# Attention of the chosen tokens: three rows of scores, six places for turned weights, and the products with V in every second head

## The chip, the cores and the metric

The kernel runs on one core of one Trainium2 chip. The metric is device time in microseconds (us) of one execution. Engines are TensorE (PE; PEld is its weight load), VectorE (DVE), ScalarE (ACT), GpSimd (POOL) and SyncE (SP).

## What is computed

One input `x` of 8192 rows by 512 goes through a layer norm; two branches work on the result and are added to `x`. The first is an attention over segments of 64 rows that carries a memory matrix from one segment to the next. The second picks the best eighth of the rows (1023 of 1024 are used) and runs a transformer block on these alone. What the change touches is the attention inside that block:

```python
q = rope(heads(hn @ wq), pos_sel)
kk = rope(heads(hn @ wk), pos_sel)
v = heads(hn @ wv)
sc = jnp.einsum('bhqd,bhkd->bhqk', q, kk) / np.sqrt(hd).astype(np.float32)
sc = sc + m_sel[:, None]
a = jax.nn.softmax(sc, axis=-1)
o = jnp.einsum('bhqk,bhkd->bhqd', a, v).transpose(0, 2, 1, 3).reshape(b, kc, d) @ wo
x1 = x_sel + o
```

There are 16 heads of 32 columns and 1023 chosen rows, padded to 1024. The multilayer perceptron of the block, with `w1` and `w2`, follows.

## The kernel before

The program has three parts one after the other: the segment attention, the chosen rows' attention with its preparation, and the perceptron. The part changed is the loop over chosen rows, from 1458.9 us to about 1808 us. Its buffers are declared from line 1743 on, its five engine programs follow until line 2127, and `mlp` comes after it.

The 1024 query rows are 8 tiles of 128 (`t` = 0 to 7), and each tile runs over 16 heads (`h`), 128 steps in all. All 1024 keys are handled at once for one head. One step is spread over three engines, each with its order written out by hand in its own `heads` function. Below, "head h" of an engine is what that engine does in iteration h of its own loop.

- TensorE, `heads` at line 2085, in this order: `score(t, h + 2)`, two products of 512 columns into the PSUM pair `Sp[h % 2]` (line 2011); then, in some heads, half of a product with V; then `turn_p(t, h - 1)`, eight transposes of the weights of head h-1 into two PSUM banks, four into `Tp[0]` (line 2019) and four into `Tp[1]` (line 2023); then, in some heads, one further piece.
- `values` is the product of four heads' turned weights with V, in two halves (`part` 0 and 1) of 32 small products each (line 2037). Group g of a tile is heads 4g to 4g+3. The halves come in heads 4g+5 and 4g+6, so two heads with products are followed by two without. Group 3 of a tile comes in heads 1 and 2 of the next one.
- The further pieces of TensorE are for the tile before: `back` in head 3, `again` in head 5 (four transposes each), `project` in head 7 (eight products of 512 columns with `wo`, line 2060), `norm_t` in head 15; and for the tile to come `stack` in heads 9, 10, 11 and 13 (four transposes each, line 2081), which makes the next tile's queries.
- VectorE, `heads` at line 1957: the reduce of head h (line 1965), which adds the mask columns to the scores, writes a row of `Sm` and takes its minimum into `least`, and then `take_t(t, h - 2)`, the copy of `Tp[1]` into a place of `PTs` (line 1916). In some heads one piece follows the copy: `weights` in head 1, `attention_rows` in head 4, `stack` in head 5 (line 1922), `second_norm` in five steps in heads 8 to 12. In the last tile `keep` comes in heads 0 to 5 and 13.
- ScalarE, `heads` at line 1861: the exponential of head h in place in `Sm` (line 1864), `take_o`, `take_t(t, h - 1)`, the copy of `Tp[0]` into `PTs` (line 1837), and in some heads a piece: `take_x1`, `take_on` in head 6, `stack` in head 3 (line 1845), `take_stack` in heads 9, 10, 11 and 13.

The waits that tie them: `score(t, h + 2)` waits until VectorE has reduced head h, since it writes over the same PSUM pair; the reduce waits for its scores and until the row of `Sm` is turned; the transposes wait for the exponential and until the copies before have emptied `Tp`; the copies wait for the transposes, and for `values` to have released their place in `PTs`:

```python
def read_before(eng, t, h):
    n = t * H + h - SLOTS
    if n >= 0:
        eng.wait_ge(s_pv, n // 4 + 1)
```

`Sm` has 4 rows of 4 KB in each partition, and `PTs` has 5 places of 4 KB. GpSimd gathers each tile's mask columns ahead by DMA, and SyncE loads the first perceptron weights during the last tile.

Of the kernel before, what the change touches and what calls it, by code (L numbers as in the profile page):

```python
# [12 lines left out]
ALU = mybir.AluOpType  # L13
ACT = mybir.ActivationFunctionType
# [10 lines left out]
P = 128  # L25
# [1227 lines left out]
def feed_forward(nc, x, maskT, positions, router_w, router_b, wq_d, wk_d, wv_d, wo_d, w1_d, w2_d, ln1, ln2,  # L1253
# [5 lines left out]
    H, DK = 16, 32  # L1259
    Q = idx.shape[1]  # L1260
    K = Q * P
    G = D // P
# [13 lines left out]
    with ExitStack() as ctx:  # L1276
        def sb(name, shape, dt=F32, c=ctx):
            return c.enter_context(nc.sbuf_tensor(name, shape, dt))
# [4 lines left out]
        ident = sb("ident2", [P, P])  # L1283
# [24 lines left out]
        mc = mcr[:, :, :].bitcast(F32)  # L1308
# [433 lines left out]
        up = Up(nc, ctx, KS, QS, xs2, x1T, Sp, w1_d, w2_d)  # L1742
        with ExitStack() as c2_:
            wo = sb("wo2", [P, G, D], c=c2_)
            Sm = sb("Sm", [P, 4, K], c=c2_)
            least = sb("least", [P, 4], c=c2_)
            rsum = sb("rsum", [P, 2, H], c=c2_)
            rinv = sb("rinv", [P, H], c=c2_)
            SLOTS = 5
            PTs = sb("PTs", [P, SLOTS, Q, P], c=c2_)  # L1750
            OTs = sb("OTs", [P, G, P], c=c2_)
            On = sb("On", [P, D], c=c2_)
# [36 lines left out]

            def slot(t, h):  # L1790
                return (t * H + h) % SLOTS

            def read_before(eng, t, h):

# [37 lines left out]
            @block.scalar  # L1832
            def _(act):
                def take_t(t, h):
                    act.wait_ge(s_t, t * (2 * H) + (2 * h + 1))
                    read_before(act, t, h)
                    act.activation(PTs[:, slot(t, h), 0:4, :], Tp[0][:, :].rearrange("p (k q) -> p k q", k=4),  # L1837
                                   ACT.Copy).then_inc(s_ta, 1)

                def take_o(t, g):  # L1840
                    act.wait_ge(s_pv, t * G + (g + 1))
                    act.activation(OTs[:, g, :], Op[:, 0:P], ACT.Copy).then_inc(s_oc, 1)

                def stack(t):
                    act.activation(qst[:, :, 0:2, :], q_rows(t), ACT.Copy).then_inc(s_qh, 1)

                def take_stack(t, g):
                    act.wait_ge(s_qp, t * G + (g + 1))
                    act.activation(QS[:, 4 * g:4 * g + 4, :], Wp[:, :].rearrange("p (h k) -> p h k", h=4),
                                   ACT.Copy).then_inc(s_qs, 1)  # L1850

                def take_on(t):
                    act.wait_ge(s_ot, t + 1)
                    act.activation(OnT[:, :, :], Wp[:, :].rearrange("p (g k) -> p g k", g=G), ACT.Copy).then_inc(s_otc, 1)

                def take_x1(t):
                    act.wait_ge(s_h2t, t + 1)
                    act.activation(x1T[:, :, cols(t)], Wp[:, :].rearrange("p (g k) -> p g k", g=G),
                                   ACT.Copy).then_inc(s_x1, 1)

                def heads(t, b, before=True, after=True):
                    for h in range(H):
                        act.wait_ge(s_sm, t * H + (h + 2))
                        act.activation(Sm[:, h % 4, 0:KC], Sm[:, h % 4, 0:KC], ACT.Exp, bias=least[:, h % 4:h % 4 + 1],  # L1864
                                       scale=-1.0, accum_out=rsum[:, b, h:h + 1]).then_inc(s_e, 1)
                        if h == 2 and before:
                            take_o(t - 1, G - 1)
                        if h in (6, 10, 14):
                            take_o(t, h // 4 - 1)
                        if h > 0:  # L1870
                            take_t(t, h - 1)
                        elif before:
                            take_t(t - 1, H - 1)
                        if h == 1 and before and t >= 2:
                            take_x1(t - 2)
                        if h == 6 and before:
                            take_on(t - 1)
                        if h == 3 and after:
                            stack(t + 1)
                        if h in (9, 10, 11, 13) and after:  # L1880
                            take_stack(t + 1, min(h - 9, 3))

                act.sem_inc(s_ta, 1)
                act.sem_inc(s_oc, 1)
                act.sem_inc(s_qh, 1)
                act.sem_inc(s_qs, G)
                heads(0, 0, before=False)
                for t in range(1, Q):
                    heads(t, t % 2, after=t < Q - 1)
                act.wait_ge(s_s, Q * H)  # L1890
                up.high(act, 0)
                take_t(Q - 1, H - 1)
                up.high_x(act, 0)
                take_x1(Q - 2)
                up.high(act, 1)
                take_o(Q - 1, G - 1)
                up.high(act, 2)
                take_on(Q - 1)
                act.activation(least[:, 0:1], rinv[:, 0:1], ACT.Gelu_apprx_tanh)
                up.high(act, 3)  # L1900
                take_x1(Q - 1)

            @block.vector
            def _(dve):
# [52 lines left out]
                def heads(t, th, b, before=True, after=True):  # L1957
                    dve.wait_ge(s_mg[b], th * 16 + 16)
                    for h in range(H):
                        dve.wait_ge(s_s, t * H + (h + 1))  # L1960
                        if before or h >= 4:

                            dve.wait_ge(s_t, t * (2 * H) + 2 * (h - 3))
                        alone(dve, s_alone)
                        dve.tensor_tensor_reduce(Sm[:, h % 4, 0:KC], Sp[h % 2][:, 0:KC], mc[:, b, 0:KC], 1.0,  # L1965
                                                 3.0e38, ALU.add, ALU.min, least[:, h % 4:h % 4 + 1])\
                           .then_inc(s_sm, 1)
                        if h > 1:
                            take_t(t, h - 2)
                        elif before:  # L1970
                            take_t(t - 1, H - 2 + h)
                            if h == 1:
                                weights(t - 1, 1 - b)
                        if h == 4 and before:
                            attention_rows(t - 1)
                        if 8 <= h < 13 and before:
                            second_norm(t - 1, h - 8)
                        if h == 5 and after:
                            stack(t + 1)
                        if not after and (h < Q - 2 or h == 13):  # L1980
                            keep(min(h, Q - 2))

# [21 lines left out]
            def _(pe):  # L2004
# [10 lines left out]
                def turn_p(t, h):  # L2015
                    pe.wait_ge(s_e, t * H + (h + 1))
                    pe.wait_ge(s_ta, t * H + (h + 1))
                    for k in range(4):
                        ins = pe.transpose(Tp[0][:, k * P:k * P + P], Sm[:, h % 4, k * P:k * P + P], ident[:, :])  # L2019
                    ins.then_inc(s_t, 1)  # L2020
                    pe.wait_ge(s_td, t * H + (h + 1))
                    for k in range(4, 8):
                        ins = pe.transpose(Tp[1][:, (k - 4) * P:(k - 4) * P + P],  # L2023
                                           Sm[:, h % 4, k * P:k * P + P], ident[:, :])
                    ins.then_inc(s_t, 1)

                def values(t, g, part):
# [58 lines left out]
                def heads(t, before=True, after=True):  # L2086
                    for h in range(H):
                        if h + 2 < H:
                            score(t, h + 2)
                        elif after:  # L2090
                            score(t + 1, h + 2 - H)
                        if h % 4 in (1, 2) and h > 2:
                            values(t, (h - 5) // 4, h % 4 - 1)
                        elif h in (1, 2) and before:
                            values(t - 1, G - 1, h - 1)
                        if h > 0:
                            turn_p(t, h - 1)
                        elif before:
                            turn_p(t - 1, H - 1)
                        if before and h == 3:  # L2100
                            back(t - 1)
                        if before and h == 5:
                            again(t - 1)
                        if before and h == 7:
                            project(t - 1)
                        if after and h in (9, 10, 11, 13):
                            stack(t + 1, min(h - 9, 3), first=not before)
                        if before and h == 15:
                            norm_t(t - 1, after)

# [21 lines left out]
class Up:  # L2132

    EARLY = 6
    SLOTS = 4
# [281 lines left out]
```

## Time and profile before

| | |
|---|---|
| median of 3 runs | 2014.53 us (2013.98 to 2016.53) |
| profiled execution: its own time | 2014.42 us |
| profiled execution: its span | 2012.7 us |
| mean granted TensorE clock | 0.968 |
| PE, DVE, ACT busy over the span | 1860.7 us (92%), 1408.4 us (70%), 880.1 us (44%) |
| the loop over heads | 1458.9 to about 1808 us |
| one inner tile of that loop (five are alike) | 42.65 us |

In a timeline row the first number is the start of an instruction or of a run of equal ones, in us from the start of the span, the second is how long it was busy, and a bracket holds the idle time of its engine before it and who ended that. Busy TensorE times run until the last result has left the array, so such rows overlap, and its pauses are about 0.17 us longer than the bracket says; the distance between two starts is the sure measure.

### The profile page before, as it was taken

Reading aid. Unit: us, or ns where it says so; the run is one execution under the profiler, and the core shown is the slowest. Engines: PE = TensorE matmul, PEld = TensorE weight load, DVE = VectorE, ACT = ScalarE, POOL = GpSimd, SP = SyncE. Lnnn points to the kernel's source line nnn. Section 1 sums busy time; section 2 is a strip of 40 time slices with the busy share of each in tenths; the row PEclk is TensorE's granted clock in tenths of the full one; section 3 lists DMA queues with packets and bytes.
Section 4 is the critical chain, followed back from the end, with each engine's and each line's share of the span. In section 5 each row is a group of like instructions: output and inputs, shape, how many; then the busy total and the mean of one; then the engine's idle time right before and its main releaser. Section 6 shows DMA issues by size and latency. Waiting matters only on the chain. (4 is left out here: it accounts for less than half of the span.)

```text
span 2012.7 us, 72288 instructions
## 1 busy us (share of the span) xinstructions
PE 1860.7 (92%) x32380; PEld 1579.4 (78%) x32380; DVE 1408.4 (70%) x3402; ACT 880.1 (44%) x1505; POOL 151.8 (8%) x187
## 2 busy tenths in 40 slices
PE   6999999999999999999999998249899999888998
PEld 6888888888888888888888886237767677667897
DVE  6777777777777777777777774577578787875222
ACT  4344343443343344434434342214587777764110
POOL 1000000000000000000000000041100000001000
PEclk9999999999999999999999998659999999999999
DMA  4112111111111111111211210215510000015000
GB/s 132 35 35 61 40 35 56 45 35 56 45 35 54 47 35 44 51 40 35 60 40 35 59 32 24 84 52 172 163 43 12 12 12 14 13 45 164 11 11 21
DMA packets 61059, 100.34 MB, mean 50 GB/s; under 512 B 4608, under 2 KB 25104, under 8 KB 60752
## 3 DMA queue, kind: packets, MB, share of 16 engines
q1 hardware_dynamic: 54976, 76.56, 12.5%
q0 software_dynamic: 5776, 19.15, 3.1%
q8 instruction: 257, 4.21, 0.9%
q14 instruction: 50, 0.41, 0.1%
HBM read 51.13 MB, written 27.26 MB: 39 GB/s over the span
## 5 line engine op out<-in xcount | busy, mean ns | idle before, releaser
L333 POOL TENSOR_TENSOR As<-T 128x512 f32<-128x512 f32 x64 | 82.6, 1290 | 1169.2 <-DVE T L611 1169.2
L1965 DVE CUSTOM_DVE_ANT_0 Sm<-Sp,mc 128x1023 f32<-128x1023 f32 x128 | 155.6, 1216 | 9.7 <-DVE r L1250 3.0
L1864 ACT ACTIVATE Sm<-Sm,least 128x1023 f32<-128x1023 f32 x128 | 146.8, 1147 | 14.0 <-DVE least L1965 13.2
L2011 PE MATMUL Sp<-KS,QS 128*128 128x512 f32 x256 | 94.3, 451 | 35.9 <-DVE least L1965 30.7
L388 ACT ACTIVATE Pq<-Pq 128x1024 f32<-128x1024 f32 x64 | 68.0, 1062 | 122.9 <-DVE Pq L580 122.9
L368 ACT ACTIVATE QT<-proj 128x512 f32<-128x512 f32 x64 | 38.1, 595 | 179.4 <-PE proj L774 179.4
L1916 DVE COPY PTs<-Tp 128x512 f32<-128x512 f32 x128 | 88.1, 689 | 40.1 <-PE Tp L2023 39.7
L351 ACT ACTIVATE DV<-proj 128x512 f32<-128x512 f32 x64 | 38.2, 597 | 159.8 <-PE proj L784 159.8
L2232 PE MATMUL Sp<-QS,KS 128*128 128x256 f32 x768 | 101.7, 291 | 6.1 <-DVE QS L2217 3.5
L2232 PEld LDWEIGHTS Sp<-QS,KS 128*128 128x128 f32 x768 | 99.8, 199 | 9.6 <-DVE QS L2217 3.9
L1837 ACT ACTIVATE PTs<-Tp 128x512 f32<-128x512 f32 x128 | 76.2, 595 | 62.1 <-PE Tp L2019 60.9
L577 DVE TENSOR_REDUCE mx<-S 128x16 f32<-128x1024 f32 x64 | 78.1, 1220 | 26.7 <-PE S L828 26.6
L2292 PE MATMUL yb<-w2m,gT 128*128 128x512 f32 x384 | 92.7, 391 | 0.0
L618 DVE TENSOR_TENSOR outt<-proj,xu 128x512 f32<-128x512 f32 x64 | 43.9, 686 | 66.0 <-PE proj L917 66.0
L774 PE MATMUL proj<-xnT_high,wq_high 128*128 128x256 f32 x512 | 85.6, 290 | 2.2 <-DVE xnT_low L516 2.2
L774 PE MATMUL proj<-xnT_high,wk_high 128*128 128x256 f32 x512 | 86.7, 291 | 0.6 <-ACT RT L372 0.6
L2011 PEld LDWEIGHTS Sp<-KS,QS 128*128 128x128 f32 x256 | 40.0, 194 | 54.5 <-issue 49.2
L2019 PE MATMUL Tp<-ident,Sm 128*128 128x128 f32 x512 | 81.9, 283 | 0.7 <-ACT PTs L1837 0.5
L774 PE MATMUL proj<-xnT_high,wq_low 128*128 128x256 f32 x512 | 82.1, 283 | 0.0
L368 ACT ACTIVATE KT<-proj 128x512 f32<-128x512 f32 x64 | 38.2, 597 | 99.9 <-PE proj L774 99.9
L774 PE MATMUL proj<-xnT_low,wq_high 128*128 128x256 f32 x512 | 81.7, 282 | 0.0
L2292 PEld LDWEIGHTS yb<-w2m,gT 128*128 128x128 f32 x384 | 70.5, 189 | 13.4
(330 smaller groups left out, 4832.7 us busy)
## 6 DMA issues: line engine op xcount, KB each, us to landing
VS<-DV SPq DMA_DIRECT2D x64, 264.0 KB, 4.0
xin<-in_x SPq DMA_DIRECT2D x32, 512.0 KB, 5.6
out_rows<-outt SPq DMA_DIRECT2D x64, 256.0 KB, 2.0
mask_columns<-x1T SPq DMA_DIRECT2D x16, 512.0 KB
xs<-in_w SPq DMA_DIRECT2D x16, 512.0 KB, 3.9
QT<-in_wqT SPq DMA_DIRECT2D x1, 1024.0 KB, 6.4
KT<-in_wkT SPq DMA_DIRECT2D x1, 1024.0 KB, 9.7
SQT<-in_wvT SPq DMA_DIRECT2D x1, 1024.0 KB, 15.4
```

The costliest lines, as they stand in the source:

```text
L333: pool.tensor_tensor(As[:, :], T1[:, :], T2[:, :], ALU.add).then_inc(s_as, 1)
L368: act.activation(raw[:, pn, 2 * k:2 * k + 2, :], v, ACT.Copy, scale=scale)
L577: link(dve.tensor_reduce(mx[:, :, :], s_half(a), AX.X, ALU.max))
L774: ins = pe.matmul(bank[:, g * BT:g * BT + BT], w[hw][:, c, o:o + P], xnT[hx][:, c, :], start=n + c == 0, stop=n == 2 and c == G - 1)
L1837: act.activation(PTs[:, slot(t, h), 0:4, :], Tp[0][:, :].rearrange("p (k q) -> p k q", k=4), ACT.Copy).then_inc(s_ta, 1)
L1864: act.activation(Sm[:, h % 4, 0:KC], Sm[:, h % 4, 0:KC], ACT.Exp, bias=least[:, h % 4:h % 4 + 1], scale=-1.0, accum_out=rsum[:, b, h:h + 1 ...
L1916: dve.tensor_copy(PTs[:, slot(t, h), 4:8, :], Tp[1][:, :].rearrange("p (k q) -> p k q", k=4))\
L1965: dve.tensor_tensor_reduce(Sm[:, h % 4, 0:KC], Sp[h % 2][:, 0:KC], mc[:, b, 0:KC], 1.0, 3.0e38, ALU.add, ALU.min, least[:, h % 4:h % 4 + 1])\
L2011: ins = pe.matmul(Sp[h % 2][:, u * 512:u * 512 + 512], QS[:, h, :], KS[:, h, u * 512:u * 512 + 512], start=True, stop=True)
L2019: ins = pe.transpose(Tp[0][:, k * P:k * P + P], Sm[:, h % 4, k * P:k * P + P], ident[:, :])
L2232: ins = pe.matmul(self.hb[n % 4][:, e * self.NT:e * self.NT + self.NT], self.w1[hw][:, c, f * P:f * P + P], self.xT[hx][:, c, :], start=m ...
L2292: ins = pe.matmul(yb[(u % 2) * QU + q][:, :], gT[hg][:, n % 4, e, q * P:q * P + P], w2[hw][:, f, :], start=f + m == 0, stop=f == FC - 1 an ...
```

## The change

The rows of `Sm` become 3 and the places of `PTs` 6, 9 blocks of 4 KB as before. A row is now found by `at(t, h)`, so that the sequence goes on over a tile's border. The halves of `values` go to every odd head: group g in heads 4g+5 and 4g+7, group 3 in heads 1 and 3 of the next tile. The pieces that depend on them go one head later on all engines: `take_o`, `back` (4), `again` (6), `project` (8), `take_on` (7), `attention_rows` (5), `second_norm` (9 to 13). TensorE's `stack` and ScalarE's `take_stack` go to heads 10 to 13; ScalarE's `stack` goes from head 3 to head 0 and VectorE's from head 5 to head 2.

```diff
-            Sm = sb("Sm", [P, 4, K], c=c2_)
+            ROWS = 3
+            Sm = sb("Sm", [P, ROWS, K], c=c2_)
-            SLOTS = 5
+            SLOTS = 6
+            def at(t, h):
+                return (t * H + h) % ROWS
...
 ACT heads
-                        if h == 2 and before:
+                        if h == 3 and before:
                             take_o(t - 1, G - 1)
-                        if h in (6, 10, 14):
+                        if h in (7, 11, 15):
                             take_o(t, h // 4 - 1)
-                        if h == 6 and before:
+                        if h == 7 and before:
                             take_on(t - 1)
-                        if h == 3 and after:
+                        if h == 0 and after:
                             stack(t + 1)
-                        if h in (9, 10, 11, 13) and after:
-                            take_stack(t + 1, min(h - 9, 3))
+                        if 10 <= h < 14 and after:
+                            take_stack(t + 1, h - 10)
...
 DVE heads
-                        if before or h >= 4:
-                            dve.wait_ge(s_t, t * (2 * H) + 2 * (h - 3))
+                        if before or h >= ROWS:
+                            dve.wait_ge(s_t, t * (2 * H) + 2 * (h - ROWS + 1))
...
-                        if h == 4 and before:
+                        if h == 2 and after:
+                            stack(t + 1)
+                        if h == 5 and before:
                             attention_rows(t - 1)
-                        if 8 <= h < 13 and before:
-                            second_norm(t - 1, h - 8)
-                        if h == 5 and after:
-                            stack(t + 1)
+                        if 9 <= h < 14 and before:
+                            second_norm(t - 1, h - 9)
...
 PE heads
-                        if h % 4 in (1, 2) and h > 2:
-                            values(t, (h - 5) // 4, h % 4 - 1)
-                        elif h in (1, 2) and before:
-                            values(t - 1, G - 1, h - 1)
+                        if h % 2 == 1 and h > 3:
+                            values(t, (h - 5) // 4, h % 4 // 2)
+                        elif h in (1, 3) and before:
+                            values(t - 1, G - 1, h // 2)
...
-                        if before and h == 3:
+                        if before and h == 4:
                             back(t - 1)
-                        if before and h == 5:
+                        if before and h == 6:
                             again(t - 1)
-                        if before and h == 7:
+                        if before and h == 8:
                             project(t - 1)
-                        if after and h in (9, 10, 11, 13):
-                            stack(t + 1, min(h - 9, 3), first=not before)
+                        if after and 10 <= h < 14:
+                            stack(t + 1, h - 10, first=not before)
```

## Rows read from the trace of the kernel before

**Rows 1.** Windows: stretch, length, busy PE, PEld, DVE, ACT, POOL; clock, DMA share, GB/s.
```profile
1500.00:1542.65 42.65, 39.46 (x452) 29.71 (x452) 34.25 (x67) 31.86 (x60) 0.94 (x1) 1.00 0.04 14
1771.80:1776.00 4.20, 4.20 (x44) 3.45 (x45) 2.88 (x6) 2.03 (x4) 0.00 (x0) 0.62 0.32 102
```

**Rows 2.** Waits from 1500 to 1542.65 us: us in total, times, longest.
```profile
DVE PTs L1916 <- PE Tp L2023: 4.7, 5, 1.2
...
PE Sp L2011 <- DVE least L1965: 2.9, 5, 0.8
```

**Rows 3.** Timeline of tile 1, heads 2 to 4.
```profile
1502.55 0.72 PE L2011 MATMUL Sp<-KS,QS 128*128 128x512 f32 x2
...
1504.70 0.60 PE L2023 MATMUL Tp<-ident,Sm 128*128 128x128 f32 x4
...
1505.05 0.71 PE L2011 MATMUL Sp<-KS,QS 128*128 128x512 f32 x2
1505.34 0.69 DVE L1916 COPY PTs<-Tp 128x512 f32<-128x512 f32 x1 [0.68 <-PE Tp L2023]
...
1507.31 0.70 PE L2011 MATMUL Sp<-KS,QS 128*128 128x512 f32 x2
...
1507.85 0.60 PE L2019 MATMUL Tp<-ident,Sm 128*128 128x128 f32 x4
...
1508.28 0.60 PE L2023 MATMUL Tp<-ident,Sm 128*128 128x128 f32 x4
```

**Rows 4.** Timeline of tile 1, heads 5 and 6.
```profile
1508.28 1.21 DVE L1965 CUSTOM_DVE_ANT_0 Sm<-Sp,mc 128x1023 f32<-128x1023 f32 x1
...
1509.42 0.69 DVE L1916 COPY PTs<-Tp 128x512 f32<-128x512 f32 x1
...
1509.65 0.70 PE L2011 MATMUL Sp<-KS,QS 128*128 128x512 f32 x2 [0.77 <-DVE least L1965]
1510.02 1.22 DVE L1922 TENSOR_TENSOR qst<-xs,qst 128x1024 fp32r<-128x1024 f32 x1
...
1511.16 1.22 DVE L1965 CUSTOM_DVE_ANT_0 Sm<-Sp,mc 128x1023 f32<-128x1023 f32 x1
...
1512.58 0.71 PE L2011 MATMUL Sp<-KS,QS 128*128 128x512 f32 x2
```

**Rows 5.** Timeline of tile 1, heads 7 to 12.
```profile
1515.09 0.72 PE L2011 MATMUL Sp<-KS,QS 128*128 128x512 f32 x2
...
1516.61 3.60 PE L2060 MATMUL Wp<-wo,OnT 128*128 128x512 f32 x8
...
1520.51 0.60 PE L2019 MATMUL Tp<-ident,Sm 128*128 128x128 f32 x4
...
1520.85 1.22 DVE L1965 CUSTOM_DVE_ANT_0 Sm<-Sp,mc 128x1023 f32<-128x1023 f32 x1
...
1522.22 0.70 PE L2011 MATMUL Sp<-KS,QS 128*128 128x512 f32 x2 [0.68 <-DVE least L1965]
...
1523.87 1.22 DVE L1965 CUSTOM_DVE_ANT_0 Sm<-Sp,mc 128x1023 f32<-128x1023 f32 x1 [0.21 <-DVE r L1246]
...
1526.96 1.22 DVE L1965 CUSTOM_DVE_ANT_0 Sm<-Sp,mc 128x1023 f32<-128x1023 f32 x1 [0.21 <-DVE r L1250]
...
1529.47 1.22 DVE L1965 CUSTOM_DVE_ANT_0 Sm<-Sp,mc 128x1023 f32<-128x1023 f32 x1 [0.21 <-DVE r L1250]
```

**Rows 6.** Timeline: head 2 of tile 2, and head 2 of tile 0.
```profile
1545.20 0.71 PE L2011 MATMUL Sp<-KS,QS 128*128 128x512 f32 x2
...
1465.37 0.84 PE L2011 MATMUL Sp<-KS,QS 128*128 128x512 f32 x2
```

**Rows 7.** Timeline of the last tile, heads 1 and 5.
```profile
1757.51 0.69 PE L2011 MATMUL Sp<-KS,QS 128*128 128x512 f32 x2 [1.76 <-DVE least L1965]
...
1771.78 0.70 PE L2011 MATMUL Sp<-KS,QS 128*128 128x512 f32 x2 [2.37 <-DVE least L1965]
...
1772.41 1.58 PE L2037 MATMUL Op<-PTs,V 128*32 128x128 f32 x32
```

More of the change, by code:

```diff
@@ L1863, in heads @@
                         act.wait_ge(s_sm, t * H + (h + 2))
-                        act.activation(Sm[:, h % 4, 0:KC], Sm[:, h % 4, 0:KC], ACT.Exp, bias=least[:, h % 4:h % 4 + 1],
+                        r = at(t, h)
+                        act.activation(Sm[:, r, 0:KC], Sm[:, r, 0:KC], ACT.Exp, bias=least[:, r:r + 1],
                                        scale=-1.0, accum_out=rsum[:, b, h:h + 1]).then_inc(s_e, 1)
-                        if h == 2 and before:
+                        if h == 3 and before:
                             take_o(t - 1, G - 1)
-                        if h in (6, 10, 14):
+                        if h in (7, 11, 15):
                             take_o(t, h // 4 - 1)
@@ L1960, in heads @@
                         dve.wait_ge(s_s, t * H + (h + 1))
-                        if before or h >= 4:
-                            dve.wait_ge(s_t, t * (2 * H) + 2 * (h - 3))
+                        if before or h >= ROWS:
+                            dve.wait_ge(s_t, t * (2 * H) + 2 * (h - ROWS + 1))
+                        r = at(t, h)
                         alone(dve, s_alone)
-                        dve.tensor_tensor_reduce(Sm[:, h % 4, 0:KC], Sp[h % 2][:, 0:KC], mc[:, b, 0:KC], 1.0,
-                                                 3.0e38, ALU.add, ALU.min, least[:, h % 4:h % 4 + 1])\
+                        dve.tensor_tensor_reduce(Sm[:, r, 0:KC], Sp[h % 2][:, 0:KC], mc[:, b, 0:KC], 1.0,
+                                                 3.0e38, ALU.add, ALU.min, least[:, r:r + 1])\
                            .then_inc(s_sm, 1)
@@ L2018, in turn_p @@
                     for k in range(4):
-                        ins = pe.transpose(Tp[0][:, k * P:k * P + P], Sm[:, h % 4, k * P:k * P + P], ident[:, :])
+                        ins = pe.transpose(Tp[0][:, k * P:k * P + P], Sm[:, at(t, h), k * P:k * P + P], ident[:, :])
                     ins.then_inc(s_t, 1)
@@ L2023, in turn_p @@
                         ins = pe.transpose(Tp[1][:, (k - 4) * P:(k - 4) * P + P],
-                                           Sm[:, h % 4, k * P:k * P + P], ident[:, :])
+                                           Sm[:, at(t, h), k * P:k * P + P], ident[:, :])
                     ins.then_inc(s_t, 1)
```

## The prediction

> **What bounds the kernel now.** I read the busy time by window first, then the waits of one inner tile, then that tile's timeline. A tile takes 42.65 us, from 1502.55 [rows 3] to 1545.20 [rows 6], at full granted clock, TensorE busy for 39.46 us of it and VectorE for 34.25 [rows 1]. So TensorE is the nearest to a bound, yet it pauses, and every pause shown is a score product waiting for VectorE's reduce, while VectorE in turn waits 4.7 us for transposes [rows 2]. The two hold each other up: which waits last depends on the order of the pieces, and that is what the change edits. The question is not how much work there is (it adds none) but how long the loop between the two is in each head.
>
> **The rules of one head, from rows.** S is the start of TensorE's head (its score product), R that of VectorE's reduce, C that of its copy, E the end of TensorE's transposes.
> - TensorE's own work: a head with products takes 2.50 us (1502.55 to 1505.05) [rows 3]; one without takes 1.40 (1507.31 to the second half of the transposes at 1508.28, plus the 0.43 that a half takes, 1507.85 to 1508.28) [rows 3]. A piece of four transposes adds 0.43: head 5 has products and `again` and takes 2.93, 1509.65 to 1512.58 [rows 4]. The head with `project` takes 4.88: transposes follow a score by 0.54 [rows 3], so the next score stood at 1520.51 - 0.54 = 1519.97, and the head began at 1515.09 [rows 5].
> - The copy starts 1.14 after the reduce (1508.28 to 1509.42) [rows 4], and not before E + 0.29 of the head before: E was 1505.05 and the copy came at 1505.34 [rows 3].
> - What follows the copy starts 0.60 later (1509.42 to 1510.02), and VectorE's `stack` adds 1.14 (1510.02 to 1511.16) [rows 4].
> - The score of the next head starts no sooner than 1.37 after the reduce (1508.28 to 1509.65) [rows 4].
>
> So behind a head with products, a head without is not 1.40 but 0.29 + 0.60 + 1.37 = 2.26 us long: 1505.05 to 1507.31 [rows 3]. In the next head the copy is ready in time, and VectorE's rhythm of 1.14 + 0.60 = 1.74 us rules, so it is shorter. Bare of all pieces, two heads with products and two without take 2.50 + 2.50 + 2.26 + 1.74 = 9.00 us; the order of the change, one and one, takes 2 x (2.50 + 2.26) = 9.52. That is the core of my forecast: alternating makes the expensive neighbour, a light head behind a heavy one, happen eight times a tile instead of four. These rules also give back the tile before head by head within 0.05 us, which is why I trust them for the one after.
>
> The Trainium skill, VectorE: DVE Perf Modes, section The DRAIN you can't avoid, says that a VectorE instruction is followed by a flush of about its duration less 0.27 us. By that figure the copy of 0.69 us would hold the next for about 0.42 more, an estimate from that page, and each light head would be about half a microsecond longer. The row disagrees: 0.60 from start to start [rows 4], and I keep it.
>
> **The change, part by part.** Rows 3 instead of 4: the reduce of h now waits for the transposes of h-3, but VectorE has just copied their result, one instruction earlier in its own queue. Nothing queues behind that wait; cost 0. Six places: a copy of h waits for the group of h-6. The second half of group g now comes in head 4g+7, ahead of the transposes of 4g+6 on TensorE, and the copy of 4g+6 needs those anyway; cost 0. With five places it would cost, so the two belong together. Nothing is added on POOL or SP, and no DMA: the mask gather still hangs on the first reduce of a tile. `back`, `again`, `project`, `take_o`, `take_on` and `attention_rows` go one head later on all engines at once, and keep their distance.
>
> Now the tile (S0 = 0; heads with products are odd). Pieces: `norm_t` in head 15 before it, so in head 0 the copy is early and 1.83 passes. S1 = 1.83, S2 = 4.33 (2.50).
> - Head 2 carries VectorE's `stack`. E of head 1 is 4.33, copy 4.62, then 0.60 + 1.14 + 1.37: S3 = 7.73, a head of 3.40. Before, `stack` lay in a head with products and `again`, which hid it wholly (1511.16 + 1.37 = 1512.53 against 1512.58) [rows 4]. This is the dearest edit: 1.14 us come into the open in each of seven tiles.
> - Heads 3 to 7: 2.50, 2.26 (with `back`, hidden), 2.50, 2.26 (with `again`, hidden), 2.50. `attention_rows`, 0.60, lies in head 5 and is covered by the products. S8 = 19.75.
> - Head 8, `project`: 4.88. S9 = 24.63. The reduce behind it starts 0.88 after that end (1519.97 to 1520.85 [rows 5]), so before, head 8, without products, lasted 2.25 (to 1522.22 [rows 5]); now head 9 has products and covers it, 2.50. This is a gain of 0.85 over a light head's 1.40.
> - Head 10: the first serial step of the norm, worth 3.02 - 1.74 = 1.28 (1520.85 to 1523.87 [rows 5]). Copy at 27.13 + 0.29; 27.42 + 0.60 + 1.28 + 1.37 = 30.67, a head of 3.54, where its own work with `stack` is 1.83.
> - Head 11: 3.09, set by the second norm step, as between 1523.87 and 1526.96 [rows 5]. Head 12: 2.50 (2.51 from 1526.96 to 1529.47 [rows 5]). S13 = 36.26.
> - Head 13: 2.93 with `stack`; the last norm step, shorter than the products, is hidden. Head 14: 1.83. Head 15: 2.93.
>
> Sum: 1.83 + 2.50 + 3.40 + 2.50 + 2.26 + 2.50 + 2.26 + 2.50 + 4.88 + 2.50 + 3.54 + 3.09 + 2.50 + 2.93 + 1.83 + 2.93 = **43.95 us** against 42.65: +1.30 a tile.
>
> ScalarE: its `stack` (1.06 us) now lies ahead of the exponential of head 1, which starts about 0.95 later. The transposes that need it have as much slack, since head 1's products lie between; I take 0. If this cover fails, up to 0.95 a tile, 6.6 in all, is the other end; below nothing it can't go, since nothing waits less. I take 0 because the copies before it end 0.1 us ahead of need by the same rules.
>
> The edges. Tile 0 has no pieces for an earlier tile; the same rules from head 2 (1465.37 [rows 6]) give its successor's head 2 at 1503.52 against 1502.55 [rows 3]: +0.97. Six steps to the last tile: 6 x 1.30 = 7.8. In the last tile `keep` rules heads 0 to 5 in both kernels; `attention_rows` moves from a light to a heavy head, and the spot where the clock fell (1771.78, behind two light heads) goes away. Worked out by the same rules its rest is 0.3 shorter. The perceptron only moves: its weight loads hang on `keep` and on what follows the loop. Total 0.97 + 7.8 - 0.3 = **+8.5 us**. Against the profiled execution's own 2014.42 that is 2022.9; the median shown is 0.1 higher, so 2023.0.
>
> **The rivals.**
> - *The clock falls in the longer waits* (slower still). New pauses of 2.0 us before head 3 and 1.7 before head 11 come in every tile. In the last tile before, a pause shown as 2.37 behind a light head was followed by half the clock (1.2 of 2.4 GHz): products of 1.58 us [rows 7], granted 0.62 over 4.20 us [rows 1], a loss of 4.20 x 0.38 = 1.6 us at most. Against it: a pause shown as 1.76 did nothing [rows 7], and mine would be shown as 1.8, with heavy heads on both sides. Once a tile it would be 7 x 1.6 = 11: 2034. Chance 0.09. The Trainium skill, Perfetto Trace Analysis, section Matmul Optimizations, speaks against the change here: products should come back to back in batches, since the engine scales with its use. The trace bears it out in that one spot only.
> - *The products cover the waits* (faster). If each light head could run on TensorE's own work, a tile would be 8 x 2.50 + 8 x 1.40 + 7 x 0.43 + 3.48 for `project` = 37.7 us, some 5 less, and the kernel about 1977; half of that, 1996. It decides from the point where the copy starts with the reduce's end instead of 0.29 behind the transposes, so if the waits for transposes [rows 2] vanish. For it: TensorE is the busiest, and 2.9 us of shown pauses are there to be had. Against it: the copy sits behind the transposes of the head just before in every light head. Chance 0.03.
> - *The moved `stack` costs nothing* (no change): if VectorE did it while it waits for transposes. Then the tile is 42.8 and the kernel 2014.5 + 0.97 - 1.14 + 6 x 0.16 = 2015.3. Against it: the queue is in order and the wait lies ahead of the copy, `stack` behind it. Chance 0.04.
>
> **How the numbers follow.** Forecast 0.84. From its bounds, 0.3 us a tile of rounding down to 2020.0, and ScalarE's cover partly gone or the clock falling in two or three tiles up to 2027.0; beyond lie the rest of the clock case and the two other signs. A measurement can tell 0.2%, 4 us, from no change; so slower 0.93, same 0.04, faster 0.03.
>
> **What would show it.** Right: five inner tiles of 43.9 to 44.0 us; TensorE's pauses before heads 3 and 11 the longest, at 1.8 and 1.5 in brackets; VectorE waiting for transposes in eight heads a tile instead of five; none before head 10. Wrong: a tile below 42.65, or light heads 2.0 us or shorter behind heavy ones; a granted clock below 1.00 in inner tiles (the first rival); transposes at line 2019 waiting for ScalarE in head 2 (its cover gone).

## The result, and the profile after

| | before | changed |
|---|---|---|
| median of 11 runs | 2014.53 us | 2024.65 us |
| lowest, highest | 2006.37, 2019.02 | 2017.43, 2030.65 |
| ratio, with 95% interval | | 1.0050 (1.0031 to 1.0069) |
| profiled span | 2012.7 us | 2024.0 us |
| the loop (first score product to the perceptron's first product) | 349.44 us | 358.90 us |
| the rest of that span | 1663.3 us | 1665.1 us |

The change makes the kernel slower by half a per cent, 10 us, against a forecast of 8.5. The median of 2024.65 us lies 1.7 above the forecast 2023.0. The last two rows matter for all that follows. The loop is short and steady, and the rest, which no edit here touches, came out between 1655.0 and 1665.1 us in the profiled executions. So the loop and its tiles are compared below, each read from the distance between two starts, and the whole time only where several runs stand behind it.

In the timeline of the changed kernel, tile 2, heads 2 and 3, this is the dearest spot of the change (line 1921 is the copy, 1927 stack, 1971 the reduce, 2017 the score):

```profile
1550.96 0.71 PE L2017 MATMUL Sp<-KS,QS 128*128 128x512 f32 x2
1551.24 0.69 DVE L1921 COPY PTs<-Tp 128x512 f32<-128x512 f32 x1 [0.68 <-PE Tp L2029]
...
1551.85 1.22 DVE L1927 TENSOR_TENSOR qst<-xs,qst 128x1024 fp32r<-128x1024 f32 x1
...
1552.98 1.22 DVE L1971 CUSTOM_DVE_ANT_0 Sm<-Sp,mc 128x1023 f32<-128x1023 f32 x1
...
1554.35 0.70 PE L2017 MATMUL Sp<-KS,QS 128*128 128x512 f32 x2 [1.71 <-DVE least L1971]
```

Read it from the top. TensorE starts light head 2 as the transposes of heavy head 1 end, and VectorE's copy follows 0.28 us later, having waited for them. Behind the copy stands stack, behind that the reduce, and only then the next score: 3.39 us for a head that [rows 3] had at 2.26 without stack. In [rows 4] the same stack stood under a head with products and cost nothing.

The waits of that tile (1546.64 to 1590.53 us) answer to [rows 2]:

```profile
DVE PTs L1921 <- PE Tp L2029: 7.1, 8, 1.2
...
PE Sp L2017 <- DVE least L1971: 4.1, 5, 1.7
```

VectorE now waits for transposes eight times a tile instead of five, once per light head, and 2.4 us longer. By window (columns as in [rows 1]), the inner tile and the one tile that is not like the others:

```profile
1546.64:1590.53 43.89, 39.51 (x456) 29.49 (x454) 34.33 (x67) 32.59 (x61) 0.95 (x1) 1.00 0.05 14
1634.40:1678.30 43.90, 39.58 (x443) 29.64 (x441) 34.03 (x65) 31.53 (x57) 0.95 (x1) 0.96 0.02 7
```

TensorE is busy for 39.5 us in both kernels: the work is the same, and the 1.23 us more (43.88 against 42.65) are waiting. The second window covers 43.90 us of a tile of 45.32, and its granted clock is 0.96. Its timeline shows where it fell:

```profile
1642.11 0.70 PE L2017 MATMUL Sp<-KS,QS 128*128 128x512 f32 x2 [1.71 <-DVE least L1971]
1642.74 1.65 PE L2043 MATMUL Op<-PTs,V 128*32 128x128 f32 x32
1644.32 1.12 PE L2025 MATMUL Tp<-ident,Sm 128*128 128x128 f32 x4
```

Behind the pause before head 3, products and transposes take 1.65 and 1.12 us instead of 1.08 and 0.66, the lower of the clock's two levels (1.2 GHz of 2.4). From one `project` to the next this tile took 45.32 us, 1.4 more than the others.

### The profile page after: what moved, and what is told of

Read it like the earlier page. It is cut to its first block and busy times, and to the rows that moved or that the text cites. A ratio compares the mean times of both kernels' runs of the same rounds, so it can differ in the third digit from the quotient of the medians.

```text
span 2024.0 us, 72286 instructions
## 1 busy us (share of the span) xinstructions
PE 1859.3 (92%) x32380; PEld 1575.2 (78%) x32380; DVE 1407.9 (70%) x3402; ACT 882.0 (44%) x1505; POOL 152.5 (8%) x187
```

## The experiments

| run | edit | inner tile | loop | span |
|---|---|---|---|---|
| before | | 42.65 | 349.44 | 2012.7 |
| changed | | 43.88 | 358.90 | 2024.0 |
| e1 | stack to head 8 | 42.75 | 352.42 | 2009.6 |
| e2 | products in pairs | 42.58 | 349.50 | 2008.0 |
| e3 | before, 3 rows and 6 places only | 42.65 | 349.38 | 2004.4 |
| e4 | changed, 5 places | 49.06 | 404.25 | 2061.1 |
| e5 | changed, again | 43.90 | 358.99 | 2018.7 |
| e6 | pairs, and stack in head 8 | 42.15 | 347.96 | 2006.2 |
| e7 | e6 with transposes ahead of products | 40.33 | 334.52 | 1995.3 |
| e8 | e1 with ScalarE's stack in head 3 | 42.93 | 353.45 | 2012.3 |
| e9 | changed, stack done twice | 46.4 to 47.6 | 379.68 | 2037.3 |
| e10 | changed, transposes ahead of products | 42.89 | 352.98 | 2009.1 |
| e11 | e10 with stack in head 8 | 42.24 | 347.39 | 2010.7 |

Inner tiles are the common value of the five of one execution, from one `project` to the next; where one of the five has a clock fall or a single longer tile it is left out (in e9 all five are given as a range). Spans are those of the profiled execution. e7 was executed six times, every other experiment once, so these are read by their tiles and loops.

**e1, stack alone.**

```diff
-                        if h == 2 and after:
+                        if h == 8 and after:
                             stack(t + 1)
```

> The changed kernel with one edit: VectorE's stack goes from head 2 to head 8, the head with project. Theory (by the rules of one head): behind the products of head 1 the 1.14 us of stack lie open in head 2, and in head 8 they lie under project; head 2 falls from 3.39 to 2.26, an inner tile from 43.88 to 42.74, and the loop (first score product to the perceptron's first product) by 6 x 1.14 = 6.8 us against 357.4 (358.9 less the 1.5 of the one clock fall), so 350.6. Rival, the three rows of scores make VectorE wait: then the tile stays at 43.9 or near. Rival, the clock: an inner tile is long only where the granted clock is below 1.00, so nothing changes in the others.

Measured: 42.75 a tile. Under `project` the whole 1.13 us vanish. Light head 2 again takes 2.26, with the copy and the pause of [rows 3]:

```profile
1548.11 0.71 PE L2017 MATMUL Sp<-KS,QS 128*128 128x512 f32 x2
1548.39 0.69 DVE L1921 COPY PTs<-Tp 128x512 f32<-128x512 f32 x1 [0.68 <-PE Tp L2029]
...
1550.37 0.70 PE L2017 MATMUL Sp<-KS,QS 128*128 128x512 f32 x2 [0.57 <-DVE least L1971]
```

Three rows of scores can't be the cause of these 1.13 us, since they are still there. The loop is 1.8 us longer than expected, and the place is known: tile 0 has no `project`, so head 8 leaves stack open there, and behind that pause, shown as 1.71, the clock fell. In e8 the same pause in the same head, 1.71 too, was followed by products of 1.08 us: no fall.

```profile
1478.00:1482.00 4.00, 2.43 (x18) 1.86 (x18) 2.97 (x5) 2.49 (x5) 0.00 (x0) 1.00 0.00 0
1482.00:1486.00 4.00, 3.86 (x41) 3.14 (x42) 1.73 (x3) 1.51 (x3) 0.00 (x0) 0.61 0.01 4
```

**e2, the products in pairs again.**

```diff
-                        if h % 2 == 1 and h > 3:
-                            values(t, (h - 5) // 4, h % 4 // 2)
-                        elif h in (1, 3) and before:
-                            values(t - 1, G - 1, h // 2)
+                        if h % 4 in (1, 2) and h > 2:
+                            values(t, (h - 5) // 4, h % 4 - 1)
+                        elif h in (1, 2) and before:
+                            values(t - 1, G - 1, h - 1)
```

> The changed kernel with the halves of the products back in heads 4g+5 and 4g+6 (1 and 2 for group 3), all else as changed. Theory: two light heads in a row cost less than two light heads each behind a heavy one, so head 3 takes about 1.74 and head 4 about 2.04, head 7 1.83; the stack's 1.14 stays open before head 3. Inner tile 42.9 against 43.88, loop about 351.5 if the clock doesn't fall. Rival, where the products stand is indifferent and only the moved stack costs: tile 43.9 still.

Measured: 42.58, 1.30 less than with products in every second head, 0.3 better than worked out; the loop of 349.50 is 2 us better. Its heads from 2 to 5, all else as changed:

```profile
1546.98 0.71 PE L2017 MATMUL Sp<-KS,QS 128*128 128x512 f32 x2
1550.37 0.70 PE L2017 MATMUL Sp<-KS,QS 128*128 128x512 f32 x2 [0.64 <-DVE least L1971]
1552.11 0.70 PE L2017 MATMUL Sp<-KS,QS 128*128 128x512 f32 x2 [0.17 <-DVE least L1971]
1553.96 0.70 PE L2017 MATMUL Sp<-KS,QS 128*128 128x512 f32 x2
```

Head 2 still takes 3.39 us, but it has products, so its pause is 0.64 and not 1.71; the light heads 3 and 4 take 1.74 and 1.85, not 2.26. So it does matter where the products stand. The pairing also puts products back into the head of stack; e6 tells the two apart.

**e3, the buffers alone.** The kernel before with `ROWS = 3`, `SLOTS = 6` and `at(t, h)`, and nothing moved.

> The kernel before with three rows of scores and six places alone, every product and piece in its old head. Theory: the rows' wait is met by the copy one instruction earlier, and the sixth place isn't needed: tile 42.65 and loop 349.4, the same as before within 0.3 us. Rival, the third row's wait costs: every head that VectorE paces gets longer, tile 43 or more.

Measured: 42.65 a tile, loop 349.38 against 349.44. The waits of tile 1 are to the digit those of [rows 2]. The buffers by themselves cost nothing and bring nothing.

**e4, five places.**

```diff
-            SLOTS = 6
+            SLOTS = 5
```

> The changed kernel with five places for turned weights instead of six. Theory: the copies of head 4g+5 now wait for the second half of group g, which comes in head 4g+7 instead of 4g+6, and the transposes and the next reduce wait behind them: about 0.95 us per group, an inner tile of 47 us (45.5 to 48). Rival, the sixth place is not needed: 43.9.

Measured: 49.06, the way that was expected, but above the range of 45.5 to 48. The waits of one of its tiles (1547 to 1596 us) show what the estimate left out: ScalarE's copies wait for the products even longer than VectorE's, and behind them stand its exponentials.

```profile
ACT PTs L1841 <- PE Op L2043: 11.2, 4, 3.8
...
DVE PTs L1921 <- PE Op L2043: 8.0, 4, 2.0
```

Without the sixth place the new order costs 5.2 us a tile more, so the two belong together, as the forecast had it.

**e5, the changed kernel again.**

> The changed kernel a second time, unedited, to see which part of its time is its own. Theory: the loop is fixed by its order, so inner tiles take 43.88 us again; TensorE's clock falls behind the pause before head 3 in some tiles and not in others (once in the first profile), at about 1.5 us each, so the loop is 357.4 plus 1.5 for each fall. Rival, the loop itself varies from run to run: tiles without a fall differ by more than 0.1.

Measured: tiles of 43.91, 43.89, 45.26, 43.90, 43.90 against 43.88, 43.89, 45.32, 43.90, 43.89. The order fixes the loop to within 0.1 us, and the clock fell once again, in the same tile. Why in that tile and not in the others, whose pauses are the same, is open.

**e6, both costs taken away.** The edits of e1 and e2 together.

> The changed kernel with both costs taken away: products in heads 4g+5 and 4g+6, and VectorE's stack in head 8. Theory: the two add up to slightly less than their sum, since with stack gone from head 2 the light head 3 becomes 2.26 and the one after 1.8; head 2 is 2.50. Worked out head by head 42.3 less the 0.3 by which the pairs run beat the same working, 42.0 us, below the 42.65 of the kernel before; the loop about 344 to 346. Rival, the two costs are one and the same: 42.6 as with either alone.

Measured: 42.15 a tile, half a microsecond under the kernel before. The four runs make a square: products in pairs or alternating, stack in head 8 or 2, give 42.15, 42.58 (pairs) and 42.75, 43.88 (alternating). Stack in head 2 costs 1.13 where head 2 is light and 0.43 where it is heavy; alternating costs 0.60 by itself and 1.30 with stack. The loop is 2 to 4 us longer than expected. One microsecond of that is another clock fall: the stretch into the last tile took 50.78 us against 49.78 in e2, which has the same order there but for stack under `project`, and the fall stands behind a pause shown as 1.77, in the last tile's head 1:

```profile
1755.22 0.70 PE L2017 MATMUL Sp<-KS,QS 128*128 128x512 f32 x2 [1.77 <-DVE least L1971]
1755.85 1.83 PE L2043 MATMUL Op<-PTs,V 128*32 128x128 f32 x32
```

In [rows 7] the same pause, 1.76, had done nothing; its products took 1.08 us.

**e7, the transposes ahead of the products.**

```diff
                         elif after:
                             score(t + 1, h + 2 - H)
-                        (products with V, as in e2)
                         if h > 0:
                             turn_p(t, h - 1)
                         elif before:
                             turn_p(t - 1, H - 1)
+                        (products with V, as in e2)
```

> e6 with TensorE's order in a head turned round: score, transposes of head h-1, then the products with V. Theory: what makes a light head long is that VectorE's copy waits for transposes that come after the products of the head before; ahead of them they end 1.1 us sooner, and the reduces then pace the light heads. Worked out head by head: 40.3 us a tile, loop 329 to 334, the kernel about 15 to 20 us under the one before. Rival, VectorE or ScalarE as a whole is the bound: nothing changes, 42.0. Rival, the products' first half now waits for nothing but the places come free a head later and the copies wait: 43 or more.

Measured: 40.33 a tile, to 0.03 as worked out, and over five rounds 1994.78 us against 2007.30, a ratio of 0.9925 (0.9908 to 0.9942). It beats both kernels. But the whole came out 12.5 us under the kernel before, not 15 to 20, and the loop of 334.52 lies just above its range of 329 to 334. Heads 2 to 4 of tile 2:

```profile
1545.73 0.73 PE L2017 MATMUL Sp<-KS,QS 128*128 128x512 f32 x2
...
1546.73 0.60 PE L2029 MATMUL Tp<-ident,Sm 128*128 128x128 f32 x4
...
1547.27 1.08 PE L2043 MATMUL Op<-PTs,V 128*32 128x128 f32 x32
1547.37 0.69 DVE L1921 COPY PTs<-Tp 128x512 f32<-128x512 f32 x1 [0.31 <-PE Tp L2029]
...
1548.28 0.73 PE L2017 MATMUL Sp<-KS,QS 128*128 128x512 f32 x2
...
1549.64 0.70 PE L2017 MATMUL Sp<-KS,QS 128*128 128x512 f32 x2
```

The copy now runs under the products, 0.9 us ahead of the next score instead of 0.28 behind it, its wait shown as 0.31 instead of 0.68, and light head 3, behind heavy head 2, takes 1.36 us, TensorE's own work. This is the mechanism of the forecast with its sign turned, and it excludes that VectorE or ScalarE as a whole was the bound. By window, TensorE is busy for 38.60 of 40.33 us:

```profile
1539.60:1579.93 40.33, 38.60 (x456) 30.40 (x452) 34.22 (x67) 32.01 (x60) 0.94 (x1) 1.00 0.05 15
```

**e8, ScalarE's stack.**

```diff
-                        if h == 0 and after:
+                        if h == 3 and after:
                             stack(t + 1)
```

> e1 with ScalarE's stack back from head 0 to head 3. Theory: the exponential that it delays has that much slack, so its place costs nothing in either head: tile 42.75 as e1. Rival, ScalarE's stack in head 0 delays the transposes: the tile falls by up to 0.95, to 41.8.

Measured: 42.93, so moving ScalarE's stack from head 3 to head 0 had cost nothing and gained 0.18. The prediction took 0, and held that below nothing it can't go; but in head 3 that stack makes heavy head 5 take 2.66 instead of 2.49, which the move takes away.

**e9, stack done twice.**

```diff
+                    link(dve.tensor_tensor(qst[:, :, 2:4, :], q_rows(t), qst[:, :, 0:2, :].bitcast(F32),
+                                           ALU.subtract))
                     dve.tensor_tensor(qst[:, :, 2:4, :], q_rows(t), qst[:, :, 0:2, :].bitcast(F32),
                                       ALU.subtract).then_inc(s_ql, 1)
```

> The changed kernel with VectorE's stack done twice in head 2, the second time behind the first. Theory: stack lies open there, so head 2 grows by the whole second instruction, 1.2 to 1.4 us with its wait; a tile without a clock fall takes 45.1 to 45.3. The pause before head 3 becomes about 3.3 us, and if long pauses are what makes TensorE's clock fall, it now falls in most tiles and not in one: then 46 to 47. Rival, stack isn't on the path: 43.9. Rival for the clock, a fall has nothing to do with this pause: one fall again at most.

Measured: head 2 takes 4.65 us, 1.26 more, so stack lies wholly on the path. In tile 2 the head behind it, with the same products, takes 3.62 instead of 2.49. From one `project` to the next the tiles take 46.38, 47.62, 47.54, 46.50 and 46.67 us, two of them above the range of 46 to 47. Tile 2 by window around the pause, and the score that ends it:

```profile
1548.00:1552.50 4.50, 4.26 (x56) 3.36 (x55) 3.85 (x7) 4.14 (x8) 0.00 (x0) 1.00 0.17 69
1552.50:1557.20 4.70, 1.77 (x14) 1.20 (x11) 4.30 (x6) 2.70 (x6) 0.00 (x0) 1.00 0.00 0
1557.20:1561.00 3.80, 3.76 (x43) 3.04 (x43) 1.64 (x3) 2.06 (x5) 0.00 (x0) 0.67 0.02 4
```

```profile
1557.24 0.70 PE L2019 MATMUL Sp<-KS,QS 128*128 128x512 f32 x2 [2.97 <-DVE least L1973]
```

Tile 1 has the same pause, ahead of the first of those distances, and no fall (line 2045 is the product with V):

```profile
1512.09 0.70 PE L2019 MATMUL Sp<-KS,QS 128*128 128x512 f32 x2 [2.96 <-DVE least L1973]
1512.72 1.08 PE L2045 MATMUL Op<-PTs,V 128*32 128x128 f32 x32
```

```profile
1507.43:1552.59 45.16, 39.53 (x456) 29.48 (x454) 35.55 (x67) 32.09 (x59) 0.94 (x1) 1.00 0.04 13
```

Its 45.16 us from head 2 to head 2 are the 45.1 to 45.3 expected without a fall, so each fall cost 1.2 to 2.5 us. Of the seven pauses shown as 2.96 or 2.97 six brought the clock down; of the seven shown as 1.70 or 1.71 in the changed kernel one did. In these runs the longer pause was followed by a fall more often, but its length alone doesn't decide it.

**e10 and e11, transposes first with the products in every second head.** The order of e7 within a head, on the changed kernel (e10) and with stack in head 8 (e11).

> The changed kernel with one edit: in TensorE's head the transposes come ahead of the products with V, which stay in every odd head; stack stays in head 2. Theory, head by head: 41.1 us a tile, plus what the copies of heads 4g+6 wait for group g, whose second half now ends behind them in head 4g+7 (about 0.3 a group, 1.2 a tile): 41.1 to 42.4. Rival, alternating is bad whatever the order within a head: 43 or more.

> e10 with VectorE's stack in head 8. Theory, head by head: 40.0 us a tile plus the same wait for places, 40.0 to 41.2; against 40.33 of e7, which has the products in pairs, it tells whether alternating is better or worse once the copies no longer wait for them.

Measured: 42.89 and 42.24, each above its range (42.4 and 41.2). The order within the head gains here too, 1.0 us on the changed kernel and 0.5 on e1, but much less than in pairs, where it gains 1.8 (42.15 to 40.33). The waits of e11 from 1500 to 1740 us show what now waits for the products:

```profile
ACT OTs L1846 <- PE Op L2043: 30.8, 23, 1.5
DVE PTs L1921 <- PE Op L2043: 22.4, 18, 1.4
```

The second half of a group now ends behind the transposes of head 4g+6, whose copies need the place that it frees; VectorE's wait for it is 1.2 us each time (22.4 / 18). The estimate of 0.3 a group was too small. ScalarE waits for the same products even longer, in `take_o`, which stands ahead of its own copy of head 4g+6. So a seventh place would free VectorE's copy but not ScalarE's. Which of the two waits costs the time was not tested, and neither were seven places nor a later `take_o`; this reason is read from the waits and is not shown.

## Why the prediction was right

**The core held.** A light head behind a heavy one took 2.26 us in heads 4 and 6 of the changed kernel, and 1.82 or 1.83 in heads 14 and 0, where the heavy head ahead has a piece of TensorE's between its transposes and the next score, as forecast; a head with products took 2.49, `stack` in head 2 made 3.39 (forecast 3.40), the norm's first step in head 10 made 3.55 (3.54), head 11 took 3.08 (3.09). The tile came to 43.88 against 43.95. e2 and e7 show the two halves of the mechanism: pair the products, and 1.30 us go; put the transposes ahead of them, and the copy's wait behind a heavy head shrinks from 0.68 to 0.31.

**One reading that didn't hold head by head.** The prediction says that its rules give back the tile before within 0.05 us in every head. They don't for `project` and the head behind it: the trace of the kernel before has the score behind `project` at 1519.64, where the prediction inferred 1519.97.

```profile
1519.64 1.02 PE L2011 MATMUL Sp<-KS,QS 128*128 128x512 f32 x2
```

So these two heads took 4.55 and 2.58 us, not 4.88 and 2.25, and in the changed kernel 4.56 and 2.82, not 4.88 and 2.50. The two errors cancel in the sum (7.38 forecast and measured), so the tile doesn't suffer.

**The edits forecast at nothing.** Rows and places: shown by e3. The need for the sixth place: shown by e4. The pieces moved one head later kept their distance. ScalarE's stack: not nothing but a gain of 0.18 (e8).

**The sum.** In the loop, +9.46 us against +8.5. Tile 0 gave 0.91 (0.97 forecast), the six steps about 1.23 each (1.30), the last tile from head 0 to its last products 51.34 against 51.60, 0.26 less (0.3 forecast). That is 8.0 of the 9.46. The other 1.5 is the one clock fall. That the whole time came within 1.7 us is partly luck: the rest of the kernel alone varies by 10 us, and the kernel before had a median of 2014.53 in these rounds and of 2007.30 in those of e7. The tile and the loop are the fair test.

**What was too sure.** The rival of the clock had 0.09, on the argument that a pause shown as 1.76 had done nothing [rows 7]. One pause that does nothing doesn't show that such pauses never do: of the seven of 1.71 in the changed kernel one brought the clock down, in each of its two profiled executions, and in e6 the very pause of [rows 7] did. The sign set out for this rival, a granted clock below 1.00 in an inner tile, came in one tile of the five. As a rival of 7 falls and 2034 us it was wrong, as a term of 1 fall and 1.5 us it belonged in the sum; the range had room for it. The page section cited there, Matmul Optimizations in Perfetto Trace Analysis of the Trainium skill, is borne out in its direction by this and by e9, where the clock was 0.67 behind the pause of 2.97.

**The bare comparison was too strong.** 9.00 against 9.52 us for four heads would be 2.1 a tile; alternating by itself cost 0.60, and 1.30 with stack (e6's square). The pieces fill pauses in one layout that they lengthen in the other, and only the walk head by head, not the bare pattern, gave the number.

## What to carry to other kernels

Where two engines hand work back and forth with single buffers, an engine's light step behind a heavy one is as long as the way round through the other engine, not as long as its own work; before spreading heavy work evenly, ask what in the heavy step the other engine waits for, and put that first in the step. A short piece on the helping engine should go under the other engine's longest step. Such a loop can be worked out from one tile's timeline with four or five distances: the tile came within 0.07 us in the changed kernel and within 0.01 to 0.32 in e1, e2, e6, e7 and e8. Where a new wait for a place in a buffer came in (e4, e10, e11), even the upper ends of the ranges were 0.5 to 1.1 us too low.

## What the runs showed of the hardware

TensorE's granted clock fell behind one of seven pauses shown as 1.70 or 1.71 us in the changed kernel, in the same tile in two executions, behind one shown as 1.77 in e6 that did nothing in the kernel before, and behind six of seven shown as 2.96 or 2.97 in e9. A fall cost 1.0 us in e6, 1.4 in the changed kernel, 1.2 to 2.5 in e9, in the heads that followed. The part of the kernel outside the loop took 1655.0 to 1665.1 us in executions with the same code for it, a swing as large as the change itself, while loops of one order agreed to 0.1 us; a single total would have told nothing here.
